# Mask products of the attention scores on quarters of the TensorE array

## The reference, cut to what matters

```python
# band: queries in blocks of W = 128, keys of the block before and of this block
band = (kj >= qi) & (kj <= qi + W)
valid = band[None] & ((nidx > 0) | (kj[None] >= W))
scores = jnp.where(valid[None, None], scores, -1e+30)
# causal
mask = jnp.tril(jnp.ones((t, t), dtype=jnp.bool_))
attn = jnp.where(mask[None, None, :, :], attn, -1000000000.0)
```

## Time and profile before

| | us |
|---|---|
| median of 3 runs | 2157.64 |
| lowest, highest | 2156.42, 2162.59 |
| the profiled execution's own time | 2152.07 |
| its span | 2150.2 |
| mean granted TensorE clock of the span | 0.936 of full |
| TensorE busy | 1789.7 (83% of the span) |
| VectorE busy | 1345.8 (63%) |
| GpSimd busy | 978.6 (46%) |
| ScalarE busy | 808.8 (38%) |

### The profile page before, as it was taken

How to read it: one execution, slowest core, us unless ns; L and a number is a source line. 1 busy time by engine, 2 the same in 40 slices (tenths; PEclk the granted TensorE clock), 3 DMA queues, 4 the chain that set the end, 5 groups by cost and what they waited for, 6 DMA issues and landing times.

```text
span 2150.2 us, 51747 instructions
## 1 busy us (share of the span) xinstructions
PE 1789.7 (83%) x21261; PEld 1250.9 (58%) x21261; DVE 1345.8 (63%) x2753; ACT 808.8 (38%) x1303; POOL 978.6 (46%) x1362
## 2 busy tenths in 40 slices
PE   4899889999999998879999997777776778888883
PEld 4566565666666666655555555667665455555553
DVE  4555555555555543574555555677876788888873
ACT  2333333333333332324444444333333444444441
POOL 3333222333332222453333435689997455555543
PEclk9999999999999999989999999888998788888886
DMA  4000000000000000023333332233443223323310
GB/s 161 1 1 1 1 2 1 1 1 1 1 1 1 1 1 1 16 56 74 64 78 71 75 75 61 60 74 78 91 87 65 46 62 65 65 65 65 65 21 8
DMA packets 167465, 89.54 MB, mean 42 GB/s; under 512 B 9393, under 2 KB 165810, under 8 KB 166978
## 3 DMA queue, kind: packets, MB, share of 16 engines
q1 hardware_dynamic: 167010, 85.70, 18.4%
q0 software_dynamic: 224, 0.54, 0.1%
HBM read 46.36 MB, written 39.85 MB: 40 GB/s over the span
## 4 chain that ended last, share of the span: by engine, by line
PE 51%; DVE 27%; ACT 7%; POOL 7%; issue 6%; DVEq 0%; POOLq 0%; ACTq 0%
PE slots L1327 38%; DVE nmx L1201 12%; PE ctx_ps L1327 10%; DVE rope_part L1242 4%; ACT probs L1087 3%; DVE rope_part L1166 2%; PE slots L1615 2%; ACT ctxT L1007 1%; DVE ctxT L1303 1%; DVE rope_part L1167 1%; POOL xn L922 1%; PE slots L1394 1%; ACT band_va L1023 1%; POOL band_rb L645 1%; DVE band_r L1167 1%
## 5 line engine op out<-in xcount | busy, mean ns | idle before, releaser
L1087 ACT ACTIVATE probs<-slots 128x1024 f32<-128x1024 f32 (+1 forms) x416 | 356.1, 892 | 322.0 <-PE slots L1327 318.8
L1201 DVE TENSOR_REDUCE nmx<-slots 128x8 f32<-128x1024 f32 (+2 forms) x352 | 407.7, 1216 | 102.8 <-PE slots L1327 101.2
L1327 PE MATMUL slots<-band_r 64*64 64x64 bf16 (+4 forms) x5120 | 393.6, 263 | 80.5 <-DVE nmx L1201 41.7
L1327 PEld LDWEIGHTS slots<-band_r 64*128 64x128 bf16 (+2 forms) x5120 | 194.6, 120 | 254.3 <-issue 129.8
L1242 DVE SCALAR_TENSOR_TENSOR rope_part<-slots,bias_qk,rope_band 128x256 f32<-128x256 f32 x512 | 212.3, 477 | 197.3 <-PE slots L1327 176.4
L1327 PE MATMUL ctx_ps<-probs,band_va 64*32 64x64 f32 (+4 forms) x5120 | 260.5, 313 | 42.3 <-issue 19.4
L986 POOL TENSOR_TENSOR band_r<-rope_part 128x512 f32<-128x512 f32 x128 | 164.5, 1285 | 250.9 <-DVE rope_part L1242 250.9
L1327 PE MATMUL slots<-mask,ident_bf 128*128 128x256 bf16 (+1 forms) x896 | 217.2, 324 | 46.9 <-DVE nmx L1201 17.7
L1327 PE MATMUL slots<-nmT,pick 64*128 64x256 bf16 (+2 forms) x2560 | 218.7, 241 | 2.7 <-issue 2.7
L1327 PEld LDWEIGHTS ctx_ps<-probs,band_va 128*32 128x32 f32 (+2 forms) x5120 | 145.3, 118 | 125.6 <-issue 62.8
L900 POOL TENSOR_TENSOR var_eps<-mean_var,eps 128x2 f32<-128x2 f32 x128 | 29.2, 228 | 393.4 <-DVE mean_var L1129 393.4
(11 more groups left out here) (181 smaller groups left out, 2947.5 us busy)
## 6 DMA issues: line engine op xcount, KB each, us to landing
band_r<-scratch SPq DMA_DIRECT2D x192, 192.0 KB, 4.5
scratch<-parts SPq DMA_DIRECT2D x96, 192.0 KB, 2.2
scratch<-parts SPq DMA_DIRECT2D x96, 128.0 KB, 2.1
scratch<-parts SPq DMA_DIRECT2D x96, 64.0 KB, 1.8
x<-in_x SPq DMA_DIRECT2D x16, 128.0 KB, 4.5
out<-x SPq DMA_DIRECT2D x16, 128.0 KB, 1.8
band_r<-in_band_qk_a SPq DMA_DIRECT2D x1, 1024.0 KB, 6.4
band_va<-in_band_qk_b SPq DMA_DIRECT2D x1, 1024.0 KB, 10.3
```

What stands on the lines that cost most here:

```text
L1087: nc.scalar.activation(probs[:, g % 2, step[2], :, 0:width], slot(u, step).rearrange("p (a n) -> p a n", a=2)[:, :, 0:width], ACT.Exp, sca ...
L1201: nc.vector.tensor_reduce(dst, src, axis=AX.X, op=ALU.max, negate=True).then_inc(free_sem(u, step), 1)
L1327: return nc.tensor.matmul(o, lhsT, rhs, start=start, stop=stop, skip_group_check=shared)
```

## The change: each mask product as two on quarters of the array

The mask product of a bank is cut into two, for output partitions 0 to 63 and 64 to 127, each with a 64x64 block of the identity. For the first bank the blocks are the upper rows with the first columns and the lower rows with the second columns. For the second bank they are the other two quarters: lower rows with the first columns, upper rows with the second. Since the operands of a row half lie in its own partitions, a second copy of the mask holds its halves swapped (`np.roll` by 64). Four products of 64*64 in four different quarters take the place of two of 128*128.

The costs that the planner uses for the steps `score` and `S` of band and causal are lower too, so the plan is laid out anew.

```diff
-        "score": [("pe", {"band": 0.78, "causal": 0.56 if i > 1 else 0.77, "chunk": 0.3, "lowrank": 0.24}.get(kind)), ("dve", 1.13)],
+        "score": [("pe", {"band": 0.55, "causal": 0.45 if i > 1 else 0.54, "chunk": 0.3, "lowrank": 0.24}.get(kind)), ("dve", 1.13)],
...
-        mask = sb("mask", [P, 2 * P], BF16)
+        mask = sb("mask", [P, 2, 2 * P], BF16)
...
-                def mm_mask(bank, heads, width, columns, allowed):
-
-
-                    o = bank.rearrange("p (h w) -> p h w", w=width)[:, :, columns]
-                    rhs = mask[:, allowed].unsqueeze(1).to_broadcast([P, heads, allowed.stop - allowed.start])
-                    mm(o, ident_bf[:], rhs, True, False, shared=True)
+                def mm_mask(bank, par, heads, width, columns, allowed):
+
+                    for half in range(2):
+                        rows, at = (slice(HALF * i, HALF * i + HALF) for i in (half ^ par, half))
+                        o = bank[at].rearrange("p (h w) -> p h w", w=width)[:, :, columns]
+                        rhs = mask[rows, par, allowed].unsqueeze(1).to_broadcast([HALF, heads, allowed.stop - allowed.start])
+                        mm(o, ident_bf[rows, rows], rhs, True, False, shared=True)
...
                         for par in range(2):
-                            mm_mask(bank(F, par), heads // 2, width, slice(width - masked, width), slice(2 * P - masked, 2 * P))
+                            mm_mask(bank(F, par), par, heads // 2, width, slice(width - masked, width), slice(2 * P - masked, 2 * P))
...
-    d["mask"] = np.concatenate([np.where(c >= r, 0.0, NEG), np.where(c <= r, 0.0, NEG)], 1).astype(bf)
+    mask = np.concatenate([np.where(c >= r, 0.0, NEG), np.where(c <= r, 0.0, NEG)], 1)
+    d["mask"] = np.stack([mask, np.roll(mask, HALF, 0)], 1).astype(bf)
```

More of the change, by code:

```diff
@@ L139, in work @@
         "v": [("pe", 1.4), ("act", 0.92)] if big else [("pe", 0.67), ("act", 0.28)],
-        "score": [("pe", {"band": 0.78, "causal": 0.56 if i > 1 else 0.77, "chunk": 0.3, "lowrank": 0.24}.get(kind)), ("dve", 1.13)],
+        "score": [("pe", {"band": 0.55, "causal": 0.45 if i > 1 else 0.54, "chunk": 0.3, "lowrank": 0.24}.get(kind)), ("dve", 1.13)],
         "parts": [("pool", 1.0)],
         "nm": [("pe", 0.12), ("act", 0.28)],
-        "S": [("pe", {"band": 0.99 if narrow else 1.74, "causal": 0.55 if narrow else 0.8, "chunk": 0.52, "lowrank": 0.48}.get(kind)),
+        "S": [("pe", {"band": 0.84 if narrow else 1.5, "causal": 0.47 if narrow else 0.7, "chunk": 0.52, "lowrank": 0.48}.get(kind)),
               ("act", 0.49 if narrow else 0.92)],
@@ L1499, in scores @@
                         for par in range(2):
-                            mm_mask(bank(F, par)[:, 0:2 * width], 2, width, slice(0, masked), slice(0, masked))
+                            mm_mask(bank(F, par)[:, 0:2 * width], par, 2, width, slice(0, masked), slice(0, masked))
                     for pair in zip(heads[0::2], heads[1::2]):
```

## The result

| | before | changed |
|---|---|---|
| median, us | 2158.32 (20 runs) | 2168.3 (20 runs) |
| profiled execution, us | 2152.07 | 2169.1 |
| its span, us | 2150.2 | 2167.3 |
| granted clock of the span | 0.936 | 0.905 |

The ratio is 1.0046, with a 95% interval of 1.0034 to 1.0057: the change is slower by about 10 us, where 24 us less were forecast. One run of the changed kernel took 4960.14 us; it counts in the 20 and not in the ratio, and without it the median is 2167.81.

What follows compares the result with a forecast made beforehand. TensorE was taken to bound the masked phases, except VectorE in the score bursts. Gains of 20.1 us in band and 6.2 in causal made 26.3, taken as 24: 2157.64 to 2134 us, range 2108 to 2160 (8 in 10).

Steps and rivals of the forecast that it cites:

- Four quarters at once, also two into one bank: In the masked fills, four mask products run as one stream: 0.32 us instead of 0.54 wide, 0.21 instead of 0.32 narrow.
- Both rivals on the bank: Masked fills: products into one bank don't overlap, 2211 us, or the four run two by two, 2173 us; together chance 0.15.
- The gain of a fill: Mask products of one fill in band and causal: a wide fill gains 0.22 us, a narrow one 0.11.
- the gain of the first fills: First `score` fill of each band unit: 0.22 less 0.095 for a change of shape, 0.125 us gained.
- The moved `V` (0): Causal units: step `V` (0), 0.79 us, now ahead of the first score fill in most units, delays VectorE's burst; sum +4.2 us.
- The other five `score` fills of a burst gain nothing, and cost nothing: Band score bursts: quicker masks after the first fill change nothing, since VectorE's 1.16 us maxima cover TensorE's 0.86 us fill.
- the clock is 0.99 and 0.98: TensorE's clock in the band and causal phases, as fractions of full, taken as its upper level, 2.4 GHz.
- The waits that I did forecast: Band bursts: TensorE's waits for `nmx` grow by about 1 us a unit, with VectorE's maxima still back to back.
- The sign that I named for band: The band phase, 781 us, becomes 20 us shorter; the prediction is wrong if mask rows shrink and it does not.
- Order and masks add up: Causal phase: 10.4 us gained by masks less 4.2 for the moved `V` (0) gives 6.2 us.
- The milder one: Masked fills: the four products run two by two, masks cost what they did, 15.2 us slower, 2173 us; chance 0.15 shared.

## Why the prediction was wrong

- **Four quarters at once, also two into one bank:** right. 0.34 and 0.24 us against 0.32 and 0.21 forecast. Both rivals on the bank are out.
- **The gain of a fill:** a little too large. What is left beside the columns is 0.13 (0.34 - 0.213, 0.24 - 0.107), not 0.105 as in the sum (0.095 + 0.01); with the whole array it was 0.11 and 0.10. With the masks issued twice the next row follows 0.56 us after the wide masks' start and 0.13 is left again (0.56 - 0.427), so it goes with the change of shape and not with the number of products. A wide fill gains 0.20 instead of 0.22, a narrow one 0.07 to 0.08 instead of 0.11. By the same sum band gains (4 x 0.20 + 4 x 0.08 - 0.19 + 0.105) x 16 = 16.6 instead of 20.1, causal (7 x 0.08 - 0.12) x 16 = 7.0 instead of 10.4. The kernel with the old order and the score masks twice, where the clock held, measured 19 us by the medians and 18 by its ratio, without the gain of the first fills.
- **The moved `V` (0):** right in its mechanism, and nearly in size. Before the quicker masks are taken off, my terms give 7 x 0.79 + 6 x 0.54 = 8.8; measured with whole-array masks 6 by the ratio and 9 by the medians, with quarters and the clock held 7 by the causal stretch. (In the sum for the even units 0.05 us have no source; that is 0.3 us in all.)
- **The other five `score` fills of a burst gain nothing, and cost nothing:** this step failed, together with the sentence that the clock is 0.99 and 0.98. I took the clock from the trace of before as given. The waits that I did forecast (TensorE waits a us more in each burst) lie where it fell. The sign that I named for band failed too: its stretch is 4.9 us shorter, where 20 were forecast. Corrected, the masks save 23.6 us and the order costs 6; measured is a loss of 10, so some 28 us are left, and the run with the masks issued twice gives back 22 of them by the medians, 25 by the ratios, although it makes each burst's first fill later again. That is the clock, above all in causal.
- **Order and masks add up:** false too. The order alone costs 6 us, in the old order quarters gain 15 by their ratio, together they lose 10. With both, the clock fell in nearly every causal unit. The moved `V` (0) does take 0.79 us of work out of the burst: in unit 21 TensorE is busy 4.87 us of the 6.88 of its maxima, against 5.71 of 7.13 in the old order. That this is how the order brings the falls is argued and not shown; in that unit itself none followed. I put the order into the sum as a delay only.
- **The rivals:** the two that slowed the kernel did so by the bank. The milder one's 2173 us lies near the measured time by luck: it had the masks keep their 0.54 us, and they took 0.34. None was on the clock, though the profile had it: 0.86 after 1300 us, where TensorE waits most, against 0.99 before.

The Trainium skill ("TensorE: Matmul & The Clock Gate", Part 1) says that the throttled state is the default one and activity releases it. The trace agrees in the direction, with 0.51 granted right behind the stretch in which TensorE was busy 2.17 of 3.40 us; the same 2.17 in the old order kept 1.00.

What stays open: what decides whether a burst brings a fall. Waits alone don't do it: with whole-array masks in the new order TensorE waits as often (61 waits for `nmx` in the causal phase, 21.5 us; after the change 55, 23.3 us) and keeps 0.99. The part of the array in use doesn't either. The time spent streaming products is a part of it at most, since 2.17 us of 3.40 went with a fall in one run and without in another; when the burst comes may be the other part, as the falls in step with the units suggest, and no run varied either by itself. It was not chance of one execution: the clock of the changed kernel's 19 comparable runs is 0.901 to 0.917, of the same quarters in the old order 0.917 to 0.924. The execution-to-execution spread follows the clock: over 19 runs of the changed kernel time and clock go together, 2159.51 us at 0.917 and 2175.41 at 0.901, about 1 us for each 0.001.

## What to carry to other kernels

Making TensorE quicker where it then waits for another engine can cost more than it gains: here its clock fell within such waits, and the price was paid by the next steps that are its own. Before such a change, look at what follows the wait and whether the granted clock there is still full; speed up the steps on the chain, and leave the covered ones as long as they are, or fill them. And undo a re-planned order separately from the edit: here it was worth 6 us alone and 24 in company. A fall right behind a stretch of little work doesn't yet show that this is its whole cause: here a burst with the same work kept its clock in the old order.

## What the hardware showed that I had not expected

- Issuing the mask products of the score fills twice made the kernel 22 us faster (2168.3 to 2145.56), at an unchanged order.
- Behind mask products on the whole array 0.10 to 0.11 us beside the columns go to the next shape, 64*128; behind those on 64*64 it is 0.13.
- From unit 22 on the clock fell in every unit, 23.9 us apart, with TensorE busy 2.17 of 3.40 us before one of the falls; in the old order a burst with the same 2.17 us kept the full clock.
- Half the array in use for the same time kept the clock (0.934 with two quarters, 0.933 with the whole array).
- With fillers in the VectorE-bound fills the mean clock of the span rose above that of before, 0.958 against 0.932.
